# Expert outputs summed on VectorE as they come; map interpolation on four column groups, with block-diagonal query and offset weights

## The reference, cut to what matters

```python
def tok(feature_map, ...):                  # deformable sampling attention, one image at a time
    q_feat = bilinear_sample(feature_map, ref)           # 32 x 32 = 1024 grid points, 64 channels
    queries = q_feat @ W_q.T
    h = gelu(layer_norm(q_feat @ W_o1 + b_o1))           # 16 wide
    off = (h @ W_o2 + b_o2) * 4                          # 8 sampling points for each grid point
    sampled = bilinear_sample(feature_map, ref + off*scale)
    keys, values = sampled @ W_k.T, sampled @ W_v.T
    return softmax(queries . keys) . values              # 8 heads of 8
def ffn(x, ...):                            # 16 experts, the two best are weighted
    top_probs, top_idx = top_k(softmax(x @ gate_w + gate_b), 2)
    hidden = silu(x @ w1[e]) * (x @ w2[e])               # for all 16 experts, 128 wide
    return sum over e of dispatch[e] * (hidden[e] @ w3[e])
h = concat(tok(x), txt)                     # 1024 + 128 = 1152 tokens
h = h + complex_scan_layer(layernorm(h))
h = h + ffn(layernorm(h))
```

## Time and profile before

| | |
|---|---|
| time, median of 3 runs | 2467.79 us (2460.09 to 2467.89) |
| the profiled execution: its own time | 2476.72 us |
| its span, first to last instruction | 2474.9 us |
| mean granted TensorE clock | 0.943 of full |
| instructions | 46859 |
| DMA | 346.85 MB, 140 GB/s over the span |

### The profile page before, as it was taken

One profiled execution on the slowest core, in us unless ns is written; L12 is line 12 of the kernel. 1 busy time (PEld: TensorE's weight loads), 2 busy tenths in 40 slices (PEclk: granted clock), 3 DMA queues, 4 the chain that ended last, 5 costly groups with the idle time before them and its releaser, 6 DMA issues.

```text
span 2474.9 us, 46859 instructions
## 1 busy us (share of the span) xinstructions
PE 2210.1 (89%) x15441; PEld 1979.4 (80%) x15441; DVE 1856.8 (75%) x4865; ACT 1399.1 (57%) x4344; POOL 1673.7 (68%) x2168
## 2 busy tenths in 40 slices
PE   2578989989999998999999899999999999989887
PEld 1566778888888888879889888888889888878776
DVE  1226888788788778888787878878787888887765
ACT  1124466566665656566565656656565666655555
POOL 0378887777686858868586877858686786867500
PEclk9967999999999999999899999989999999989989
DMA  9575636356472736538272745638173563712100
GB/s 221 148 207 154 182 104 186 113 164 173 110 217 66 213 97 177 167 106 222 77 212 85 198 138 152 186 95 225 52 221 108 166 175 109 201 52 68 49 3 6
DMA packets 362993, 346.85 MB, mean 140 GB/s; under 512 B 49152, under 2 KB 313472, under 8 KB 362624
## 3 DMA queue, kind: packets, MB, share of 16 engines
q1 hardware_dynamic: 313600, 209.57, 31.4%
q0 software_dynamic: 49152, 134.28, 18.6%
HBM read 205.87 MB, written 137.89 MB: 139 GB/s over the span
## 4 chain that ended last, share of the span: by engine, by line
PE 58%; issue 11%; DVE 11%; ACT 10%; POOL 8%; DMA 2%; ACTq 0%; DVEq 0%; another core or an unknown queue 0%; POOLq 0%
PE bank_o L634 16%; PE bank_h L624 8%; PE bank_d L700 7%; PE bank_h L625 7%; PE bank_d L690 7%; POOL gath L570 5%; ACT scaled L831 5%; PE bank_a L727 5%; PE bank_a L712 2%; POOL rest L577 2%; DMA gath<-table,idx 2%; DVE hid L967 2%; DVE wsam L1062 1%; PE bank_p L655 1%; PE bank_a L741 1%
## 5 line engine op out<-in xcount | busy, mean ns | idle before, releaser
L570 POOL DMA_INDIRECT gath<-table,idx x1024 | 1110.6, 1085 | 267.2 <-issue 238.5
L831 ACT ACTIVATE scaled<-bank_o,disp 128x64 f32<-128x64 f32 x2304 | 502.2, 330 | 370.8 <-PE bank_o L634 334.4
L624 PE MATMUL bank_h<-xsplit,w 128*128 128x384 f32 x1536 | 634.7, 413 | 83.3 <-ACT silu L780 52.9
L634 PEld LDWEIGHTS bank_o<-w_sb,hid 128*128 128x128 f32 x4608 | 567.9, 197 | 10.1 <-DVE hid L967 9.6
L634 PE MATMUL bank_o<-w_sb,hid 128*128 128x64 f32 x4608 | 563.8, 278 | 6.3 <-DVE hid L967 6.2
L625 PE MATMUL bank_h<-xsplit,w 128*128 128x384 f32 x1536 | 539.0, 351 | 0.0
L780 ACT ACTIVATE silu<-bank_h 128x384 f32<-128x384 f32 x768 | 393.8, 514 | 122.0 <-PE bank_h L625 104.2
L967 DVE TENSOR_TENSOR hid<-silu,bank_h 128x384 f32<-128x384 f32 x768 | 416.8, 548 | 53.4 <-ACT silu L780 38.5
L577 POOL MEMSET rest<- 1x400 f32 x1024 | 432.1, 422 | 29.6
L624 PEld LDWEIGHTS bank_h<-xsplit,w 128*128 128x128 f32 x1536 | 307.6, 200 | 139.5 <-ACT silu L780 68.0
L1062 DVE TENSOR_TENSOR wsam<-gath,cw 128x1024 f32<-128x1024 f32 x256 | 312.6, 1221 | 115.4 <-PE bank_d L690 54.7
(11 more groups left out here) (141 smaller groups left out, 2306.2 us busy)
## 6 DMA issues: line engine op xcount, KB each, us to landing
table<-pixmaj SPq DMA_DIRECT2D x80, 1024.0 KB
xin<-x_dram SPq DMA_DIRECT2D x256, 256.0 KB
table<-pixmaj SPq DMA_DIRECT2D x32, 960.0 KB
table<-pixmaj SPq DMA_DIRECT2D x16, 1088.0 KB
gath<-table,idx POOLq DMA_INDIRECT x1024
out_dram<-ob SPq DMA_DIRECT2D x48, 96.0 KB
gath<-w_dram SPq DMA_DIRECT2D x4, 512.0 KB, 8.8
interp_sb<-interp_dram SPq DMA_DIRECT2D x1, 1024.0 KB, 5.3
```

The lines of the kernel that those rows point to most:

```text
L570: pool.indirect_dma_start(out=gath[buf][:, p, :, :].rearrange("p a c -> p (a c)"), out_offset=None, in_=table[par], in_offset=bass.Indirec ...
L624: mm(bank[:, 0:GC], w12[:, e, which, 0, :], xsplit[gp][:], start=True, stop=False)
L634: last = mm(bank_o[n % 2][:, C * i:C * (i + 1)], hid[:, e, 128 * k:128 * (k + 1)], w3_sb[:, e, :], start=True, stop=True)
L831: last = nc.scalar.activation(scaled[n % 2][:, i, :], bank_o[n % 2][:, C * i:C * (i + 1)], ACT.Identity, scale=disp[gpar(par, g)][:, k, e: ...
```

## The change

Two parts of the kernel are rewritten, and all the order strings are laid out anew for them.

*Experts.* W now goes by expert: for expert e, three matmuls (one for each token tile) into 192 columns of `bank_o[n % 2]`. ScalarE's scaling is gone. Z is, for each expert, three `scalar_tensor_tensor` instructions of 128 x 64 on VectorE, which read the bank, multiply by the column of `disp` and add to the running sum in `ob` (for e = 0 to `h2`). The sum of tile k waits for the same tile's sum of the expert before. `scaled`, `part`, the pairwise adds and M2 on VectorE go away; `hid` has 4 places (`HB`) in place of 16, and X's product waits until the W of four experts before is made.

*Map.* A2 has its operands exchanged: the interpolation weights (128 x 32) are stationary, the map row (128 x 64) moves, and the result is [32 points, 64 channels] at one of four places `tile_position=(0, 32*a)` of the array's columns, for four grid rows. All 1024 points now fit one bank. ScalarE copies it to `qf_sb`; a new step A3 turns it in four transposes of 128 x 128; ScalarE copies that to `qfT`, in which two token tiles stand above each other. B0 and B1 then take 4 matmuls each, over 128 partitions, with `w_q` and `w_o1` laid twice on the diagonal of `w_blk`.

```diff
+HB = 4
-    ("A2", "act"): [(3,), (7,)],
+    ("A2", "act"): [(i,) for i in range(7, 8)],
+    ("A3", "pe"): [()],
+    ("A3", "act"): [()],
-    ("M2", "dve"): [(i,) for i in range(3)],
-    ("W", "pe"): [(0, 0, 0), (0, 0, 1), ...
+    ("W", "pe"): [(i, j) for i in range(3) for j in range(16)],
-    ("Z", "dve"): [(0, 0, 0), (0, 0, 1), ...
+    ("Z", "dve"): [(i, j) for i in range(3) for j in range(16)],
 ORDER = {
...
-        w_q = sb("w_q", [C, C])
-        w_off1 = sb("w_off1", [C, LH])
+        w_blk = sb("w_blk", [128, 2 * C + 2 * LH])
-        qfT = sb("qfT", [C, NQ])
+        qf_sb = sb("qf_sb", [128, QT * C])
+        qfT = sb("qfT", [128, QT // 2, 128])
-        hid = sb("hid", [128, NE, GC])
-        scaled = [sb(f"scaled{i}", [128, 8, C]) for i in range(2)]
-        part = sb("part", [128, 2, GT, C])
+        hid = sb("hid", [128, HB, GC])
...
+        block_loads += [(w_blk[C * p:C * (p + 1), C * p:C * (p + 1)], wq) for p in range(2)]
+        block_loads += [(w_blk[C * p:C * (p + 1), 2 * C + LH * p:2 * C + LH * (p + 1)], w_o1) for p in range(2)]
...
                     elif kind == "W":
-                        g, half, k = args
-                        n = 2 * GT * (NGRP * b + g) + GT * half + k
-                        pe.wait_ge(hid_done, SLOTS * b + NE * g + 8 * half + 8)
-                        wait(pe, eo_scaled, n - 1)
-                        for i in range(8):
-                            e = 8 * half + i
-                            last = mm(bank_o[n % 2][:, C * i:C * (i + 1)], hid[:, e, 128 * k:128 * (k + 1)],
+                        g, e = args
+                        n = SLOTS * b + NE * g + e
+                        pe.wait_ge(hid_done, n + 1)
+                        wait(pe, eo_added, GT * (n - 1))
+                        for k in range(GT):
+                            last = mm(bank_o[n % 2][:, C * k:C * (k + 1)], hid[:, n % HB, 128 * k:128 * (k + 1)],
                                       w3_sb[:, e, :], start=True, stop=True)
                         last.then_inc(eo_ready, 1)
...
-                        if n == 4:
-                            pe.wait_ge(qf_stored, 2 * b + 1)
-                        for i in range(4 * n, 4 * n + 4):
-                            for r in range(2):
-                                row = FIRST_ROW[i] + r
-                                last = mm(bank_a[0:C, NG1 * (i % 16):NG1 * (i % 16 + 1)],
-                                          pixmaj[:, C * row:C * (row + 1)], interp_sb[:, i, r, :],
-                                          start=r == 0, stop=r == 1)
+                        for r in range(2):
+                            for a in range(4):
+                                row = FIRST_ROW[4 * n + a] + r
+                                last = mm(bank_a[NG1 * a:NG1 * (a + 1), C * n:C * (n + 1)], interp_sb[:, 4 * n + a, r, :],
+                                          pixmaj[:, C * row:C * (row + 1)], start=r == 0, stop=r == 1,
+                                          tile_position=(0, NG1 * a))
...
+                    elif kind == "A3":
+                        pe.wait_ge(qf_stored, b + 1)
+                        for m in range(QT // 2):
+                            last = mm(bank_a[:, 128 * m:128 * (m + 1)], qf_sb[:, 128 * m:128 * (m + 1)], eye[:],
+                                      start=True, stop=True, is_transpose=True)
+                        last.then_inc(qfT_ready, 1)
                     elif kind == "B0":
-                        pe.wait_ge(qf_stored, 2 * b + 2)
-                        for t in range(QT):
-                            last = mm(bank_a[:, C * t:C * (t + 1)], qfT[:, 128 * t:128 * (t + 1)], w_q[:],
+                        pe.wait_ge(qfT_stored, b + 1)
+                        for m in range(QT // 2):
+                            last = mm(bank_a[:, 128 * m:128 * (m + 1)], qfT[:, m, :], w_blk[:, 0:2 * C],
                                       start=True, stop=True)
                         last.then_inc(q_ready, 1)
...
-                    elif kind == "W":
-                        g, half, k = args
-                        n = 2 * GT * (NGRP * b + g) + GT * half + k
-                        act.wait_ge(eo_ready, n + 1)
-                        act.wait_ge(disp_done, NGRP * b + g + 1)
-                        wait(act, pair_sum, n - 1)
-                        for i in range(8):
-                            e = 8 * half + i
-                            last = nc.scalar.activation(scaled[n % 2][:, i, :], bank_o[n % 2][:, C * i:C * (i + 1)],
-                                                        ACT.Identity, scale=disp[gpar(par, g)][:, k, e:e + 1])
-                        last.then_inc(eo_scaled, 1)
...
-                        if e % 8 == 0:
-
-                            wait(dve, eo_ready, 2 * GT * (NGRP * b + g - 1) + GT * (e // 8 + 1))
+                        wait(dve, eo_ready, n - HB + 1)
                         r = (2 * (NE * g + e) + 1) % 3
-                        tt(hid[:, e, :], silu[e % 2][:], bank_h[r][:, 0:GC], ALU.mult).then_inc(hid_done, 1)
+                        tt(hid[:, n % HB, :], silu[e % 2][:], bank_h[r][:, 0:GC], ALU.mult).then_inc(hid_done, 1)
                     elif kind == "Z":
-                        g, half, k = args
-                        n = 2 * GT * (NGRP * b + g) + GT * half + k
-                        sums.start(n)
-                        dve.wait_ge(eo_scaled, n + 1)
-                        eo = scaled[n % 2]
-                        for m in (4, 2):
-                            link(sums, tt(eo[:, 0:m, :], eo[:, 0:m, :], eo[:, m:2 * m, :], ALU.add))
-                        tt(part[:, half, k, :], eo[:, 0, :], eo[:, 1, :], ALU.add).then_inc(pair_sum, 1)
-                    elif kind == "M2":
...
+                        g, e = args
+                        gp = gpar(par, g)
+                        n = SLOTS * b + NE * g + e
+                        dve.wait_ge(eo_ready, n + 1)
+                        if e == 0:
+                            wait(dve, out_done[gp], 8 * NGRP * b + 8 * (g - gp))
+                        for k in range(GT):
+                            if e:
+                                dve.wait_ge(eo_added, GT * (n - 1) + k + 1)
+                            stt(ob[gp][:, k, :], bank_o[n % 2][:, C * k:C * (k + 1)], disp[gp][:, k, e:e + 1],
+                                (ob[gp] if e else h2[g])[:, k, :], ALU.mult, ALU.add).then_inc(eo_added, 1)
```

More of the change, by code:

```diff
@@ new lines @@
+        "FlGFyGFFhGilmGmFlGFGFGFlGFmsGmtFGFulGFGFGFaalGFmGFmwGlFGFyGFGFGFlaGmFGmFGFlGFGFFaGaalmaGmFalGsFtGFuG",
+        "FlGFmGFmwGFalyGFGFaGFaGFlGamFGmFGFlsGFtaGFaGFlaumGFmaGFblbGFbbbGFblwbmbGmFGlFyGFcGFGFdlGFmGFmeGFlGFs",
+        "GtFGFGulFhGmiFGmFGlFaaGalFwmGFmGFyGFlGaFGaFaaaGFGFGFGFlsGFtmGFmGFulGFGlFaGFmGFmwGFlGFylGFGmFaGmFaGFl",
+        "GFaGlFamGFsmGtFaGlFaGFuFGalGFmbbmGFbbGbFbwbGFblGFylGFcGmFGmFdGFlGFelGFmGFsmGtFGlFGFluhGiFmGFmGFaaGFw",
+        "GaFaGFyFGaGFaGaaFGFGFlGFGFlsGFtmGFmGFulGFGlFaGFmGFmwGFlGFylGFGmFaGmFaGFlGFaGFlaGmFsmGtFaGlFaGFuFaGbl",
@@ new lines @@
+        "HyGDHzGHGrHkGHGHksGtHGHkGHmGHmGnHukvGHGHxGHkmGHmwnGkHGHyGHzGHmkGrHmGnHGHksGtHGHmGkmHnBGHCkGHuGvHGmHD",
+        "xmGnHkGHwGHkGHyGHzGkHmGrHmGnkHGeHsGtHGmkHfGmHnGHhGHkuGvHjmGHxmGnHBGHwGHCGHyGDHzGHGrHkGHGHksGtHGHkGHm",
+        "GHmGnHukvGHGHxkGHmGHmwnGkHGHyGHzGHmkGrHmGnHGHksGtHGHGmkmHnGBHGHuvGkHCGHmDxmGnHkGHwGHGkHyGHzGHmGrkHmG",
+        "nHGHsGtHGkHGHGHmGkHmunvGHGHxGkHGHwGHGHmymGnHBzGHCGDHrGHGHsGtHGHGHGHGHuvGHGHxGHGHwGHGHyGHzGHGrHGHGHsG",
+        "tHGHGHGHGHuvGHGHxGHGHwGHGHyGHzGHGHGHGHGHGHGHGHGHGHGHGHGHGHGHGHGHGHHH",
@@ L395, in build @@
         qf_stored = sem("qf_stored")
+        qfT_ready = sem("qfT_ready")
+        qfT_stored = sem("qfT_stored")
         q_ready = sem("q_ready")
@@ L475, in gpar @@
             return (NGRP * p + g) % 2
-        def n_odd(g, half, k):
-            return (2 * GT * g + GT * half + k) % 2
         @block.sync
@@ L554, in _ @@
             nc.gpsimd.memset(w_kv[:], 0.0).then_inc(setup_p, 1)
+            nc.gpsimd.memset(w_blk[:], 0.0).then_inc(setup_p, 1)
             nc.gpsimd.memset(neghalf[:], -0.5).then_inc(setup_p, 1)
@@ L739, in run @@
                         pe.wait_ge(q_stored, b + 1)
-                        for t in range(QT):
-                            last = mm(bank_a[:, LH * t:LH * (t + 1)], qfT[:, 128 * t:128 * (t + 1)], w_off1[:],
+                        for m in range(QT // 2):
+                            last = mm(bank_a[:, 2 * LH * m:2 * LH * (m + 1)], qfT[:, m, :], w_blk[:, 2 * C:2 * C + 2 * LH],
                                       start=True, stop=True)
@@ L840, in run @@
                                 wait(act, table_out[q], 32 * b)
-                            wait(act, qf_ready, 2 * b)
+                            wait(act, qf_ready, b)
                         dst = view(pixmaj[:], 4 * c * C, [[C, 4], [C * HW // 2, 2], [1, C]])
```

(15 more changed lines are left out.)

182 lines of the change are left out of this document (83 added, 99 removed), and 8 rows, old and new, of the table KINDS.

## The result

The changed kernel takes 2310.44 us, the median of 4 runs (2306.16 to 2315.57), against 2466.61 for the kernel before in its 4 runs: 0.9373 of it, interval 0.9345 to 0.9401, 156 us faster. Measured again as after_again, beside other runs, the same kernel gave 0.9377 (0.932 to 0.9434). The forecast was 2410 with a range from 2350 to 2485: right in its sign, too small by a factor of 2.7.

What follows compares the result with a forecast made beforehand. TensorE, 94% busy in the pipelined middle, was taken as the bound. TensorE -49 (85% of 58), ScalarE -20, VectorE +20 and end -8 gave -57 us: 2468 - 57 = 2411, said as 2410, range 2350 to 2485.

Steps and rivals of the forecast that it cites:

- the map -49 us: TensorE's map matmuls: -31 us from B0, B1 and A3, -27 from A2, together -58, of which 85% counted.
- ScalarE -20: Scaling leaves ScalarE (-502.2 us busy); of TensorE's 53.7 us of waits on `silu`, 20 us gained, between 0 and 54.
- end -8: Last image, three groups without gathers: 91.6 us become 75, at most -17, taken as -8.
- B0, B1 and A3: Map matmuls on TensorE: B0 gains 1.31 us, B1 1.09, A3 adds 0.46; net -1.94 us an image, -31 over 16.
- the failed step of the TensorE sum: A2's 2048 records with operands exchanged: 0.045 us each, halfway between overlap and none, -27 us; full overlap -59.
- What a shorter TensorE list is worth: Of TensorE's 58 us saving 85% counts, since the rest falls into stretches where it waits anyway.
- VectorE: too low in busy time: 2304 Z instructions at 0.145 us: 334 us in, 304.7 out, +29 net; 20 us more TensorE waits (0 to 150).
- The signs of being wrong: Middle: VectorE above 90% and naming most of the chain, or TensorE waiting longer for Z than it did for `silu`.
- The start: Start of the kernel: two more small loads and one memset, +1 us, within the noise.
- rival 1: Column places overlap fully and the waits on `silu` go: -141 us at the most, typically 2350 us; chance 0.09.
- Rival 4: A2: switching column places stalls each of 1024 matmuls by half of 0.3 us, +150 us, about 2570; chance 0.05.
- rival 3: Z in the middle: VectorE becomes the bound at 0.25 us an instruction, +271 us busy, 95%, about 2525; chance 0.13.

Runs made afterwards that it cites:

- map_only: The kernel before with only the map part changed (A2 on four column places, A3, B0 and B1), experts and their order as before: 2420.28 us, 0.9845 of before.
- one_group: The changed kernel with the same interpolation matmuls reordered so that each piece of A2 stays at one column place: 2347.31 us, 0.9549 of before.
- full_shape: The changed kernel with g_in and xnT zero-filled to 128 partitions, so the scan layer's second matmul is 128*128: 2311.87 us, 0.9346 of before.
- experts_only: The changed kernel with the old map, the copy of the grid's first half put into ScalarE's list: 2394.05 us, 0.9719 of before.
- act_scale: The changed kernel with scaling by disp back on ScalarE, by expert, and Z one 192-column addition on VectorE; full computation: 2300.04 us, 0.9294 of before.
- z_three_adds: The changed kernel with a tensor_tensor addition replacing each 64-column scalar_tensor_tensor, leaving out the gate weighting: 2270.19 us, 0.9177 of before.
- z_one_add: The changed kernel with one 192-column tensor_tensor addition replacing the three scalar_tensor_tensor, leaving out the gate weighting: 2243.9 us, 0.9128 of before.

## Why the prediction was wrong, step by step

*Which step failed.* By parts, the prediction gave the map -49 us (85% of 58) and the experts with the end -8 (-20 + 20 - 8). Alone, the map is worth 38 us (0.9845 of 2467) and the experts are worth 69 (0.9719); the remaining 49 of the 156 come only with both together, some 41 of them at the start (462 against 421 us). So the experts' part is the step that failed first of all, in the terms "ScalarE -20" and "end -8". The map's -49 is near 38 by luck: its saving was put too low and the share of it that shows too high, as told below. And the start was put at nothing.

*B0, B1 and A3: right.* Predicted -1.94 us an image. In the timeline of the changed kernel (weight loads, as the earlier trace rows):

```profile
1373.98 0.48 PEld L736 LDWEIGHTS bank_a<-eye,qf_sb 128*128 128x128 f32 x4
1374.43 0.19 PEld L628 LDWEIGHTS bank_h<-xsplit,w 128*128 128x128 f32 x1
...
1378.88 0.97 PEld L742 LDWEIGHTS bank_a<-w_blk,qfT 128*128 128x128 f32 x8
1379.77 0.19 PEld L628 LDWEIGHTS bank_h<-xsplit,w 128*128 128x128 f32 x1
```

A3 takes 0.45 and B0 0.89 us from its first load to the next step's, without a stall ahead; 0.46 and 0.93 were forecast.

*A2: the failed step of the TensorE sum.* "If loading stays the limit, 0.058 x 32/64 = 0.029: 2048 x 0.029 = -59 us" was the price of full overlap, and -27 was taken. Loads at different places don't queue: a record costs 0.014. A2's matmuls are busy 50.6 us in all:

```profile
L728 PE MATMUL bank_a<-pixmaj,interp_sb 128*32 128x64 f32 x2048 | 50.6, 234 | 0.8 <-ACT pixmaj L839 0.8
```

and 146.3 before: -96 us. The bound was made from how one place behaves, and it priced only the load. The Trainium skill, TensorEngine Tiling (Key Properties), has tiles run loads and matmuls in parallel; by that the 0.054 of one place becomes 0.054/4 = 0.0135, an estimate, and the trace agrees with 0.014. The prediction read it as "the loads would be the limit", and that was the mistake.

*What a shorter TensorE list is worth: wrong.* 85% was counted. map_only took 8 us an image off the list (A2's and B's loads) and won 3.0 in the middle, 38%; there the wait for `hid` before X grew from 6.2 to 29.8 us (window 421 to 2000), and the one for `silu` stayed (38.1 and 37.6). one_group shows 2.3 of 5.1, and full_shape none of 1.8. At the start the same edit is worth 18 us. Two errors of opposite sign meet: the list got shorter by 128 us in place of 58, and of that 38 us showed without the experts' part, 85 with it (0.9719 to 0.9373, 41 of them at the start). The prediction looked only for room on TensorE and VectorE. GpSimd, which it read as 74% of the middle, wasn't weighed, and it held 8% of the chain of waits then and 17% now.

*ScalarE: -20 us, too small.* The prediction took 20 of 53.7 us of waits. In the window from 421 to 2000 us they fall from 47.6 to 1.3 us in experts_only and to 3.8 in the changed kernel, so nearly all of them went. In act_scale, where three scalings of a W and not eight stand ahead of `silu`, 23.7 are back. That fits the reading that an in-order list with 1.75 us of scaling ahead of `silu` (502.2 us over 288 steps) made them. But the waits that go aren't the gain: TensorE's idle time fell by 1.9 us an image in experts_only and rose by 1.3 in the changed kernel, where waits for VectorE stand in their place. What gives the experts' part its other 3.5 us an image, the finer W, the new order, the additions that are gone or the clock, isn't separated by any run. act_scale shows that the move of the scaling, by itself, gives none of it.

*VectorE: too low in busy time, in effect within its range.* Forecast 0.145 us an instruction, 334 us in all; measured 0.220, 507 us. The multiply by a column is the difference of 60 ns (z_three_adds), which L1132, with a full tensor as its second operand, doesn't show. Net VectorE gained 139 us of load: less than 507 - 305 = 202, because instructions of different lines run side by side for 215 us of the span, 158 before. At 0.3 us for each us, z_one_add's rate, that is some 40 us of loss, an estimate; 20 was taken, of a range to 150. The waits for Z stay small: 30 us at L637 over the whole run, where the matmuls of before waited 53 us for `silu`. The signs of being wrong were "VectorE in the middle above 90%" together with "most of the chain", or longer waits for Z than for `silu`. Neither came in full: VectorE is at 92.7% but holds 27% of the chain against TensorE's 40%. What did grow are TensorE's other waits for VectorE: 82.4 us for `wsam` at L693, and 35.5 for `hid` at L628, where before had 33.2 and 27.7. By the figures of the Trainium skill, VectorE: DVE Perf Modes (TRN2 errata), the prediction's estimate was 192 ns and 442 us; the trace has 275 ns and 507 us, and a plain addition from PSUM at 216 ns, so it agrees in neither. Its net figure, +137, is close to the 139 measured, but those come from 507 us and that overlap, so the trace doesn't bear the figures out.

*The end: too small.* -8 was taken, of -17 at most for the last three groups. From the fourth last store to the last, three groups take 76.5 us now, against 91.6: -15 (experts_only 76.9, map_only 91.6). In the last group the timeline shows TensorE without a gap:

```profile
2285.09 0.78 PE L637 MATMUL bank_o<-w_sb,hid 128*128 128x64 f32 x6
...
2286.46 0.78 PE L637 MATMUL bank_o<-w_sb,hid 128*128 128x64 f32 x6
```

One expert takes 1.37 us, near the 1.32 of the prediction. That W fills the time in which X waited for `silu` and the product is a reading of this, not tried. The other 30 us lie in the groups before these, from the last A2 on, which the prediction didn't count: experts_only has 38 of the 45 us there.

*The start: 14 to 21 us, forecast +1.* The first images run without experts beside them, so the map's chain from A2 to the gathers is on the path. The first gather starts at 89.7 us in the changed kernel and in map_only and at 102.6 before, the first of the second image at 212 and 209 against 231. TensorE's clock is low in this stretch (0.90 before, 0.87 after, against 0.96 and 0.97 in the middle); what that costs there wasn't tried. map_only shows 18 us. The prediction read only the middle and the end.

*The rivals.* The result lies beyond rival 1 (-141 at most). Its mechanisms, full overlap of the places and no waits for `silu`, both happened. Rival 4, a stall on changing the place, is refuted by distances of 0.007 us (its sum also reads 2468 + 150 - 31 = 2587, not 2570); rival 3 had its condition (VectorE over 90%, 0.22 us an instruction) without its outcome. Its 95% puts the whole run's 271 us into a stretch of 13.4 of the 16 images; it should read 93%.

## What to carry to other kernels

A float32 matmul with 32 stationary columns is worth packing by four column places even where it has to be turned and copied once more: a record costs a quarter. If an engine has a long step ahead of a short one on the critical loop, try it in shorter pieces where it is before you move it to another engine: here the two came out alike (act_scale and the changed kernel). Don't count the waits that go as the gain: others took their place, and TensorE's idle time an image rose. When two engines are both above 90%, neither list is worth its full length: here a us of VectorE was worth 0.3 us, and a us of TensorE in the middle between none and 0.45. Look for the third engine too: with its gathers and the gaps between them GpSimd was at 91%, and by the chain of waits it came next when VectorE was relieved.

## What the runs showed of the hardware that wasn't expected

Loads of the stationary operand at four column places overlap: 16 loads of 0.11 us each start within 0.16 us. `scalar_tensor_tensor` with a per-partition column takes 275 ns for 128 x 64 where `tensor_tensor` takes 216, both from PSUM; with a full tensor and an immediate at 128 x 128 it takes 283.
